# The third slot tile of an expert: two column halves on two halves of the partitions, one transpose, turned rows in blocks of 64

## The reference

```python
capacity = int(CAPACITY_FACTOR * T * K / E)                # 320 slots per expert
logits = xf @ gate_w.T
probs = jax.nn.sigmoid(logits)
top_vals, sel = jax.lax.top_k(probs, K)                    # K = 2
weights = top_vals / (top_vals.sum(-1, keepdims=True) + 1e-06)
...
padded = jnp.zeros((sentinel + 1, d), xf.dtype).at[slot].set(x_rep)
padded = padded[:sentinel].reshape(E, capacity, d)         # 16 x 320 x 256
h = jax.nn.gelu(jnp.einsum('ecd,edf->ecf', padded, w1), approximate=False)      # w1: 256 x 512
out_padded = jnp.einsum('ecf,efd->ecd', h, w2).reshape(sentinel, d)             # w2: 512 x 256
...
out = (gathered * weights.reshape(-1)[:, None]).reshape(T, K, d).sum(axis=1)
x = x + jnp.tanh(g_ffn[0]) * out
```

## Time and profile before

| | us |
|---|---|
| median of 3 runs | 340.29 |
| lowest and highest | 338.02 and 340.69 |
| the profiled execution, by the clock of the runs | 339.9 |
| span of the profiled execution, first to last instruction | 338.2 |
| mean granted TensorE clock | 0.968 of full |
| busy in the span: PE, PEld | 308.3, 267.3 |
| busy in the span: DVE, ACT, POOL | 251.2, 207.9, 191.4 |
| expert stage, from the first turn to the end | 186 to 338.2 |

### The profile page before, as it was taken

How to read it: one execution, slowest core, us unless ns; L and a number is a source line. 1 busy time by engine, 2 the same in 40 slices (tenths; PEclk the granted TensorE clock), 3 DMA queues, 4 the chain that set the end, 5 groups by cost and what they waited for, 6 DMA issues and landing times. The chain is left out here.

```text
span 338.2 us, 6265 instructions
## 1 busy us (share of the span) xinstructions
PE 308.3 (91%) x2077; PEld 267.3 (79%) x2080; DVE 251.2 (74%) x585; ACT 207.9 (61%) x570; POOL 191.4 (57%) x242
## 2 busy tenths in 40 slices
PE   8989999999999999998849999999999999999800
PEld 3646779988888888887724899999999999999700
DVE  2679887698989898989755398888888888887200
ACT  2646877887888888866461376666666666665300
POOL 8034566585777777788771023555555555566650
PEclk9999999999999999999978999999999999999965
DMA  6989999700111111111224737878787878853440
GB/s 159 274 241 292 182 167 152 195 19 16 49 49 55 57 57 64 56 51 62 78 95 149 249 104 201 204 205 208 204 216 211 224 202 220 211 82 43 48 46 8
DMA packets 40906, 45.68 MB, mean 135 GB/s; under 512 B 5461, under 2 KB 34666, under 8 KB 40874
## 3 DMA queue, kind: packets, MB, share of 16 engines
q1 hardware_dynamic: 33410, 35.78, 39.3%
q0 software_dynamic: 7424, 9.48, 15.6%
q10 hardware_dynamic: 40, 0.02, 0.0%
HBM read 28.02 MB, written 17.24 MB: 134 GB/s over the span
## 5 line engine op out<-in xcount | busy, mean ns | idle before, releaser
L554 POOL DMA_INDIRECT out_dram<-wqT,diag x48 | 73.3, 1528 | 77.4 <-DMA out_dram<-wqT,diag 43.4
L1370 PE MATMUL ps_scores<-value_t,score_t 128*128 128x320 f32 x384 | 59.1, 310 | 0.0
L1370 PEld LDWEIGHTS ps_scores<-value_t,score_t 128*128 128x128 f32 x384 | 56.5, 188 | 0.4 <-DVE value_t L1079 0.3
L1269 PE MATMUL ps_out<-value_t,pT 128*128 128x256 f32 x384 | 53.3, 289 | 0.9 <-DVE pT L968 0.9
L1240 PE MATMUL ps_scores<-score_t,xn 128*128 128x512 f32 x192 | 53.9, 426 | 0.0
L1269 PEld LDWEIGHTS ps_out<-value_t,pT 128*128 128x128 f32 x384 | 47.7, 189 | 1.7 <-issue 1.6
L1240 PEld LDWEIGHTS ps_scores<-score_t,xn 128*128 128x128 f32 x192 | 36.4, 190 | 6.8
L713 ACT ACTIVATE ps_scores<-ps_scores 128x640 f32<-128x640 f32 x30 | 20.6, 688 | 34.2 <-PE ps_scores L1370 34.1
L460 POOL DMA_INDIRECT padded<-z,slot_row x32 | 33.4, 1043 | 10.0 <-issue 7.1
L640 ACT ACTIVATE probs<-ps_scores,row_low 128x64 f32<-128x64 f32 x128 | 38.0, 327 | 0.5 <-DVE row_low L941 0.5
L1093 DVE CAST value_t<-ps_scores 128x640 fp32r<-128x640 f32 x30 | 24.7, 824 | 18.0 <-ACT ps_scores L713 17.8
(11 more groups left out here) (210 smaller groups left out, 690.0 us busy)
## 6 DMA issues: line engine op xcount, KB each, us to landing
raw<-in_L_ffn_w_dram SPq DMA_DIRECT2D x16, 512.0 KB, 4.8
wo_sb<-in_L_ffn_w_dram SPq DMA_DIRECT2D x16, 512.0 KB, 3.5
padded<-empty SPq DMA_DIRECT2D x2, 2064.0 KB, 31.0
diag<-padded SPq DMA_DIRECT2D x16, 258.0 KB, 4.9
out_dram<-x SPq DMA_DIRECT2D x16, 128.0 KB, 1.7
padded<-empty SPq DMA_DIRECT2D x1, 1032.0 KB, 34.1
diag<-padded SPq DMA_DIRECT2D x16, 64.5 KB, 4.7
wq_sb<-in_L_xattn_Wq_dram SPq DMA_DIRECT2D x2, 512.0 KB, 8.0
```

The source lines that it names most:

```text
L554: pool.indirect_dma_start(out, bass.IndirectOffsetOnAxis(ap=xg[0:SLOTS[k], r, k, TOKEN:TOKEN + 1].bitcast(U32), axis=0), y[0:SLOTS[k], j, ...
L1269: op = pe.matmul(ps_attn, pT[:, a, c], mv, start=c == 0 and (a, b) == PARTS[0], stop=c == HC - 1 and (a, b) == PARTS[-1])
L1370: op = pe.matmul(ps_scores[:, f, 0:CAPACITY], w1_hl(p, a)[:, c, f * P:(f + 1) * P], x_hl(p, b)[:, c], start=c == 0 and (a, b) == PARTS[0], ...
```

## The change

- `fetch`: the third slot tile's second DMA takes columns 128 to 257 of the 64 rows (130 numbers, 520 bytes a row) to partitions 64 to 127, starting at column 0 of `xg`, instead of the last two numbers. `y_low` finds its weight at column `WEIGHT - P` of these partitions.
- `turn`: the first two slot tiles are transposed as before, but each result of 128 slots goes to two blocks of 64. The third slot tile, now with its first column half on partitions 0 to 63 and its second on 64 to 127, is transposed at once, 128x128: 5 transposes, all of 128 rows.
- The turned x lies in 640 columns of PSUM in one piece (`ps_rows`, the same two banks): five blocks of 64 slots, and within each block first the 64 columns of column half 0, then those of half 1. The copies at lines 701 and 1079 take the 640 in one run.
- `first_product` reads column half c through `x_part`: five runs of 64 columns, 128 apart, instead of 320 in one run. The output is the same 320 columns.

```diff
         def x_hl(p, k):
             n, at = DC * CAPACITY, 4 * FC * CAPACITY
-            return value_t[:, at + (2 * p + k) * n:at + (2 * p + k + 1) * n].rearrange("p (c s) -> p c s", c=DC)
+            return value_t[:, at + (2 * p + k) * n:at + (2 * p + k + 1) * n]
+
+        def x_part(p, k, c):
+
+            return x_hl(p, k).rearrange("p (b c s) -> p c b s", c=DC, s=SLOTS[2])[:, c]
...
+        ps_rows = ps_pT[:, :, :].rearrange("p a n -> p (a n)")
...
-                    sp.dma_start(xg[SLOTS[2]:, r, 2, TOKEN:], padded[at + 2 * P:at + CAPACITY, TOKEN:]).then_inc(fetched[r], 16)
+                    sp.dma_start(xg[SLOTS[2]:, r, 2, 0:ROW - P], padded[at + 2 * P:at + CAPACITY, P:]).then_inc(fetched[r], 16)
...
-                    act.activation(x_hl(j, 0), ps_pT[:, :, 0:CAPACITY], ACT.Copy).then_inc(x_high, 1)
+                    act.activation(x_hl(j, 0), ps_rows[:, 0:DC * CAPACITY], ACT.Copy).then_inc(x_high, 1)
...
-                                   scale=xg[SLOTS[2]:, e % GATHERS, 2, WEIGHT:WEIGHT + 1]).then_inc(y_lowered, 1)
+                                   scale=xg[SLOTS[2]:, e % GATHERS, 2, WEIGHT - P:WEIGHT - P + 1]).then_inc(y_lowered, 1)
...
-                    dve.tensor_tensor(x_hl(j, 1), ps_pT[:, :, 0:CAPACITY], x_hl(j, 0).bitcast(F32), ALU.subtract).then_inc(x_low, 1)
+                    dve.tensor_tensor(x_hl(j, 1), ps_rows[:, 0:DC * CAPACITY], x_hl(j, 0).bitcast(F32), ALU.subtract).then_inc(x_low, 1)
...
-                    for k in range(SLOT_TILES):
-                        m = SLOTS[k]
+                    for k in range(SLOT_TILES - 1):
+                        to = ps_rows[:, k * DC * P:(k + 1) * DC * P].rearrange("p (b c s) -> p c b s", c=DC, s=SLOTS[2])
                         for c in range(DC):
-                            op = pe.transpose(ps_pT[:, c, k * P:k * P + m], xg[0:m, t % GATHERS, k, c * P:(c + 1) * P], ident[0:m, 0:m])
-                    op.then_inc(xg_turned, 1)
+                            pe.transpose(to[:, c], xg[:, t % GATHERS, k, c * P:(c + 1) * P], ident[:, :])
+                    k = SLOT_TILES - 1
+                    pe.transpose(ps_rows[:, k * DC * P:DC * CAPACITY], xg[:, t % GATHERS, k, 0:P], ident[:, :]).then_inc(xg_turned, 1)
...
-                                op = pe.matmul(ps_scores[:, f, 0:CAPACITY], w1_hl(p, a)[:, c, f * P:(f + 1) * P],
-                                               x_hl(p, b)[:, c], start=c == 0 and (a, b) == PARTS[0],
+                                op = pe.matmul(ps_scores[:, f, 0:CAPACITY].rearrange("p (b s) -> p b s", s=SLOTS[2]),
+                                               w1_hl(p, a)[:, c, f * P:(f + 1) * P], x_part(p, b, c), start=c == 0 and (a, b) == PARTS[0],
```

## The result

The changed kernel took 357.06 us (median of 4 runs, 356.09 to 358.42), the kernel before beside it 339.93 (4 runs, 338.02 to 340.69): a ratio of 1.052, 95% interval 1.049 to 1.055. It is 5% slower where 1.15% faster was forecast. The profiled execution took 358.42; its span is 356.6, 18.4 longer than before.

What follows compares the result with a forecast made beforehand. TensorE was taken to pace SyncE's bursts, and these the scatters, with the last four groups running free. Eleven turns at 0.35 (3.85), plus 0.15, less 0.1 for the fetch, gave 3.9: 340.3 to 336.4 us, range 334.8 to 340.8.

Steps and rivals of the forecast that it cites:

- Turn: TensorE's transposes of one expert's gathered rows: 0.93 us before, forecast 0.58, so 0.35 saved per expert.
- 24 loads: Weight loads of an expert's first product on TensorE: forecast to take 3.53 us still, with the moving operand in blocks.
- bursts: SyncE's DMA issues per expert (w2, w1, gathered rows): forecast 7.85 us apart instead of 8.20, paced by TensorE.
- blocks and fetch: Moving operand in five runs of 64 columns, taken as 0; larger third DMA of rows, taken as 0.1 us, paid once.
- Rival C: TensorE's turn: the stop isn't of the 64-row form and stays; only one load goes, giving 339.0 us; chance 0.08.
- D: First product's moving operand: blocks cost time, 350.2 us at the full bound; chance 0.12.
- The 0.11: Chance given to a slower kernel, all of it from blocks costing time in the moving operand.
- the 0.35: Time in us saved per expert in TensorE's turn: 0.11 for the load that goes, the rest for the 64-row pair.
- from bursts to scatters: Each GpSimd scatter group starts about 9.2 us behind SyncE's burst; a late group doesn't push the next.
- Rival B: GpSimd's scatters don't follow the bursts; their chain keeps its own 8.20 us, only its start moves: 339.4 us; chance 0.20.
- The sign: What would show the forecast wrong: TensorE beginning to wait at line 1399 for ScalarE's first result at line 729.
- its 0.19 of cover: Time in us left between ScalarE's result at line 729 and TensorE's third product; if gone, up to 0.1 a loop lost.

## Why the prediction was wrong

**The terms were right.** Turn 0.59 (0.58 forecast), 24 loads in 3.54 (3.53), bursts 7.86 apart (7.85), blocks and fetch at nothing. Rival C needed a turn of 0.8 and D loads of over 3.6; both fell with the first rows of the trace. The 0.11 that I gave to a slower kernel was all D's, so it named the outcome and not the cause. The rule of the Trainium skill's page TensorE: Matmul & The Clock Gate that stood against the 0.35 (section LDWEIGHTS) falls with C: the turn lost 0.34, not 0.107.

**The step that failed** is the one from bursts to scatters: "The reader is to see ... the late group doesn't push the next one", and from it "as each group hangs on its burst, this is paid once, not per expert". I read from one late group that a group stands 9.2 behind its burst whatever happened before. The reading just ahead of it, that scatters issued behind a burst wait for it, stands up (5.3 to 5.9 behind weights, 2.4 to 2.6 without); what I didn't ask is what happens when the third scatter falls behind the next burst. A group hangs on its burst only while three margins last, none of which I had priced: 0.50 from the third scatter to the split of w1 (at expert 2), 1.45 from its end to the next weights (225.59 and 227.04 before; 225.32 and 225.18 after the change), and the time by which expert e - 2 has landed before the fetch of expert e + 3 and the y buffer of expert e need it. The burst, the split and the next burst move with TensorE, and the scatters follow only in part: the first margin shrank from 0.93 to 0.51 at expert 1 and from 0.50 to less than nothing at expert 2. Once it was gone the long scatter used up the second. What the runs show in place of a group that hangs on its burst is a loop that closes over the landing: a late landing holds back the next scatters and the next weights alike, 10.7 per expert. A group that was 9.70 behind its burst, which I took as harmless, had 0.62 left to the split (289.74 and 290.36). That the 2 slow executions of 19 went over this edge is likely but not shown: no trace of them is kept.

**Rival B** had half of it. The chain of scatters doesn't follow bursts at 7.87 where it stood in this loop: 9.17 and 10.99 from expert 2 on. But it has no clock of its own at 8.2: with the burst held later it keeps 7.88, and B's 339.4 supposes that a chain slower than the bursts does no harm. It does: it falls behind until the weights of the next burst and the splits stand in its way. I had looked for a new wait in TensorE's own work only.

**The sign was named, for the wrong reason.** "The forecast would also be wrong if TensorE began to wait at line 1399 for line 729": it does, 10 times, up to 3.13. But the cause isn't that its 0.19 of cover was gone: line 734 (729 before) itself waits up to 5.3 for a landing. I had followed that wait forward to TensorE and not backward to what releases it.

**The gain** of 0.33 per expert is there where the loop runs at TensorE's pace (7.88 against 8.20, experts 6 to 11 of one trace), and the price of getting there in this kernel is as large as the gain.

## What to carry to other kernels

Before you make the pacing engine faster, list for each asynchronous chain beside it (here scatter, landing, next scatter) how much time lies between its events and the ones that come with the faster engine, and compare that with what the change takes off per iteration; here the chain had 0.50 and 0.62 to spare at experts 2 and 10, and the change took 0.34 per expert. Ask also what one late event of the chain holds back: here it released the scatters and the weights that delay them, so the loop stayed slow. A kernel that is now and then 5% slower may have such a second rhythm: look at it before you tune. And a prefetch that is released as early as possible isn't always best: one wait that ties it to a place in the loop gave back 15 of the 17 lost, though the same wait cost the kernel before 5 to 6.

## What the runs showed of the hardware

A GpSimd scatter that starts while VectorE subtracts with two SBUF inputs (128x1024, 1.22 long) takes up to 1.06 longer (2.48 instead of 1.42 at most for a third one). 150 that had begun before it took 1.62 at most, and the three beside a subtraction with a PSUM input 1.56, 1.56 and 1.42. The Trainium skill, page SBUF — State Buffer, section Who interferes with whom, says that a VectorE instruction with two SBUF inputs contends with a GpSimd instruction that reads SBUF. The runs agree, if the scatter counts as one that reads (its row numbers lie in SBUF). The same section infers that building DMA descriptors isn't held up by `tensor_tensor`. This scatter as a whole is: 1.84, 2.21, 2.08 against 1.56, 1.56, 1.42. No run separates its reading of the row numbers from its building of descriptors, so the inference itself is neither confirmed nor refuted.

A moving fp32 operand in five runs of 64 columns costs TensorE nothing: 3.54 for 24 matmuls of 320 columns, 3.53 in one run.

A stop of 3.13 cost TensorE more than itself: the 24 loads behind it took 5.00 instead of 3.54, and behind a stop of 2.51 (ended at 281.85) 4.46. But behind stops of 2.61 and 2.80 (ended at 249.65 and 303.24) they took 3.53 and 3.54 with a granted clock of 1.00, and behind one of 1.25 (271.38) 3.54. So the length of the stop alone doesn't tell whether the clock falls.
